# Memory projections: the substitution's last four heads move from GpSimd to VectorE

## What is computed

```
k = k / max(norm(k), 1e-12)
alpha = sigmoid(alpha_raw) * 0.5
def t_step(M, kv):
    Mk = einsum('bhde,bhe->bhd', M, k_t)
    forget = Mk[..., :, None] * k_t[..., None, :]
    write = v_t[..., :, None] * k_t[..., None, :]
    return M - alpha * forget + beta * write
```

## Time and profile before

| | |
|---|---|
| median of three runs | 4661.99 us |
| the profiled execution, its own time | 4658.4 us |
| its span, first to last instruction | 4656.7 us |
| mean granted TensorE clock | 0.885 |
| VectorE busy in the span | 2542.6 us (55%) |
| GpSimd busy in the span | 1687.9 us (36%) |
| the stage, from its first wait to the next stage's first work | about 2541 to 2954 us |

### The profile page before, as it was taken

The page is one execution under the profiler, slowest core; times in us unless marked ns, Lnnn a source line. Parts: engine busy times, 40 slices in busy tenths (PEclk is TensorE's granted clock), DMA queues, the critical chain, the costliest instruction groups (busy, mean ns, idle before and its releaser), DMA issues. The chain is left out here.

```text
span 4656.7 us, 53980 instructions
## 1 busy us (share of the span) xinstructions
PE 3691.3 (79%) x17563; PEld 1661.0 (36%) x17563; DVE 2542.6 (55%) x3976; ACT 1439.1 (31%) x2018; POOL 1687.9 (36%) x1362
## 2 busy tenths in 40 slices
PE   8899999979997899965892330376787966999994
PEld 3322222223333333334551220132445534555553
DVE  5599999935551355534325779655663694111113
ACT  2257777743332233321232210011442210111111
POOL 0132222236663166641560457333441322222221
PEclk9989999989998999987895665687887977999997
DMA  4542232211104411024226111233333103333333
GB/s 172 185 69 68 62 74 63 49 53 37 43 19 134 140 37 37 26 78 133 67 86 214 54 54 36 64 89 95 106 117 110 36 27 101 95 90 104 95 90 81
DMA packets 323882, 382.96 MB, mean 82 GB/s; under 512 B 52016, under 2 KB 252992, under 8 KB 322688
## 3 DMA queue, kind: packets, MB, share of 16 engines
q1 hardware_dynamic: 270912, 285.83, 19.8%
q0 software_dynamic: 35776, 73.97, 6.3%
q10 hardware_dynamic: 17024, 20.97, 1.3%
HBM read 240.69 MB, written 135.76 MB: 81 GB/s over the span
## 5 line engine op out<-in xcount | busy, mean ns | idle before, releaser
L571 DVE TENSOR_REDUCE modulated_mx<-modulated_ring 128x1 f32<-128x512 f32 x1024 | 651.9, 684 | 52.0 <-PE modulated_ring L478 46.4
L555 ACT ACTIVATE modulated_probs<-modulated_scores 128x1024 f32<-128x1024 f32 x512 | 496.1, 1021 | 182.4 <-PE modulated_scores L499 182.3
L2843 DVE TENSOR_TENSOR expert_h<-expert_gelu,expert_bank 128x512 f32<-128x512 f32 x128 | 88.1, 688 | 390.2 <-PE expert_bank L2811 390.2
L2771 POOL DMA_INDIRECT scratch_acc<-expert_y,expert_idx x64 | 101.0, 1579 | 483.7 <-DVE expert_y L2848 441.6
L508 PE MATMUL modulated_acc<-modulated_probs,modulated_v 128*32 128x512 f32 x2048 | 273.6, 606 | 0.6 <-ACT modulated_probs L555 0.6
L499 PE MATMUL modulated_scores<-modulated_q,modulated_k 128*128 128x512 bf16 x1024 | 268.3, 384 | 1.3 <-DMA modulated_q<-modulated_turned 0.7
L478 PE MATMUL modulated_ring<-modulated_k,modulated_q 64*128 64x512 bf16 x1024 | 239.6, 399 | 34.1 <-DMA modulated_v<-scratch_v 22.7
L910 POOL TENSOR_TENSOR causal_total<-causal_total,causal_probs 128x1024 f32<-128x1024 f32 x96 | 225.6, 2350 | 86.5 <-ACT causal_probs L831 85.5
L910 POOL TENSOR_TENSOR meta_total<-meta_total,meta_probs 128x1024 f32<-128x1024 f32 x96 | 225.6, 2350 | 86.6 <-ACT meta_probs L831 85.6
L2811 PE MATMUL expert_bank<-expert_xT,expert_wg 128*128 128x512 f32 x512 | 243.2, 597 | 7.8 <-ACT expert_xT L2823 7.8
L853 DVE TENSOR_REDUCE meta_mx<-meta_maxima 128x2 f32<-128x1024 f32 x120 | 146.0, 1217 | 184.4 <-PE meta_maxima L737 184.4
(11 more groups left out here) (471 smaller groups left out, 7057.2 us busy)
## 6 DMA issues: line engine op xcount, KB each, us to landing
expert_wg<-x_WgT SPq DMA_DIRECT2D x16, 1024.0 KB, 4.8
expert_wu<-x_WuT SPq DMA_DIRECT2D x16, 1024.0 KB, 6.8
expert_wd<-x_WdT SPq DMA_DIRECT2D x16, 1024.0 KB, 5.4
modulated_k<-scratch_k_part SPq DMA_DIRECT2D x192, 64.0 KB, 2.9
modulated_q<-scratch_q_part SPq DMA_DIRECT2D x192, 64.0 KB, 3.0
scratch_v<-proj_v SPq DMA_DIRECT2D x8, 1024.0 KB, 6.6
modulated_v<-scratch_v SPq DMA_DIRECT2D x16, 512.0 KB, 4.4
scratch_M<-steps_snap SPq DMA_DIRECT2D x16, 512.0 KB, 3.2
```

The source lines that it names most:

```text
L555: nc.scalar.activation(probs[u % NPROBS][i][:], sc[i][:], ACT.Exp, scale=SCALE).then_inc(s_exp, 1)
L571: V.tensor_reduce(mx[h % 2][:, x // 2, 1 - j % 2, j // 2, x % 2:x % 2 + 1], ring[bank_of["max", 4 * m + j]][:], AX.X, ALU.max).then_inc(s_ ...
L2771: added[j].done(G.indirect_dma_start(out=scr["acc"], out_offset=bass.IndirectOffsetOnAxis(ap=idx[j][a][:], axis=0), in_=y[j][:, a, :], in_ ...
```

## The change

VectorE's second part becomes all 8 heads of the second half, and GpSimd's third part goes, with its 30 instructions a group, its waits for the copy and for the scaled A, and SP's wait for GpSimd. The number of VectorE's instructions stays; those of the second part have twice the elements.

```
-        pool_s = st.steps("pool", [("far", n) for n in range(len(far))] + [(x, i) for i in range(SUB - 1, 0, -1) for x in ("share", "rows")])
-
-        PARTS = ((0, 0, HP), (1, 0, HP // 2), (1, HP // 2, HP))
+        pool_s = st.steps("pool", [("far", n) for n in range(len(far))])
+
+        PARTS = ((0, 0, HP), (1, 0, HP))
...
                 dve_s.wait(sp, g, ("rows", 1, 1))
-                pool_s.wait(sp, g, ("rows", 1))
                 for half in range(HH):
...
                     pool_s.done(products(nc.gpsimd, other[n % 2], i, hp), ("far", n))
-                act_s.wait(pool, g, "copy")
-                dve_s.wait(pool, g, ("scaled", 1))
-                for i in range(SUB - 1, 0, -1):
-                    pool_s.done(share(nc.gpsimd, other[0], i, PARTS[2]), ("share", i))
-                    pool_s.wait(pool, g, ("share", i))
-                    pool_s.done(add(nc.gpsimd, other[0], i, PARTS[2]), ("rows", i))
-                    pool_s.wait(pool, g, ("rows", i))
```

## The result

The changed kernel took 4641.65 us in the median of five runs (4634.66 to 4644.94), the kernel before, run beside it, 4662.17. The ratio is 0.9941, with a 95% interval of 0.9927 to 0.9956, that is 20 to 34 us less. In a second comparison the medians were 4637.09 and 4668.23 (ratio 0.9941, 0.9927 to 0.9955). Forecast were 32.0 us less, a size inside that interval. The median of 4641.65 itself lies 1.65 us above the high end of the forecast (4640); put as the ratio on the 4661.99 that the forecast started from, it is 4634.5, inside the range.

A forecast was written before the change was run, and what follows sets the result against it. No one engine bounds the program, but VectorE alone bounds the substitution, slowed by GpSimd. 27.0 us from the substitution plus 5.0 from the early load make 32.0, so 4662.0 - 32.0 = 4630.0 us; range 4622 to 4640.

The forecast's parts named there:

- The substitution: VectorE's substitution, all heads on VectorE without GpSimd: 68.2 us a group instead of 81.66, 27.0 us less in both groups.
- The early load: GpSimd's load of the second group's input, issued near 2665 instead of 2738.82, inside the first substitution: worth 5.0 us.
- the landing: Second group's input load, from GpSimd's issue to arrival: 8.6 us as before, so near 2674, inside the substitution.
- ScalarE's wait for the q store: Second group: ScalarE's copy of quad two's q waits some 7 us for the first quad's q store; now comes last.
- the slow restart of TensorE: TensorE idles over 50 us, then starts slowly a second time after the substitution: 1.85 us more on kv matmuls.
- quad three at T + 16.8: TensorE's kv matmuls of the second group's third quad start 16.8 us after the substitution's end (T), instead of 21.8.
- The rival in which the load is starved: GpSimd's early load lands only once VectorE's two-input instructions end: 12.6 us gained in all, 4649; chance 0.02.
- the two terms: VectorE's shorter substitution, 27.0 us in both groups, and the second group's early load, 5.0 us: 32.0 us.
- the 25 to 36 us of the prediction: Sign: wrong if the second substitution's end, counted from the stage's start, comes under 25 or over 36 us earlier.
- Slow long instructions: Substitution rows 15 to 9: long instructions cost 2.01 ns an element by themselves, 47.4 us slower, 4709; chance 0.03.
- A gain given back later in the program: The stage's end waits for something unseen or the next stage starts no earlier: 4662; chance 0.03.

The follow-up runs named there:

- with the order fixed: A wait added so that VectorE's product always goes ahead of GpSimd's next: 4623.92 us on the changed kernel, 4654.26 on the kernel before.
- the second and the third pair of profiles: Both kernels unchanged, each profiled twice more: products of pairs 69.53 to 69.67 us a group in all four executions.
- the first pair: The first profiles of the kernel before and the changed one: memset of A to end of second substitution 397.5 and 379.8 us.
- dve_alone: Changed kernel with VectorE always first, the last four heads' substitution left out, VectorE's old instructions alone: substitution 52.21 us a group, program 4588.60 us.

## Why the prediction was right, and where it was not

**The substitution.** Forecast were 68.2 us, measured 68.20 and 68.21. The price of 1.04 ns an element and 0.07 us an instruction, taken from the short rows that ran alone and from the 1664-element product, holds for the long ones. No row gives the 0.11 us an instruction that the high end of the range allowed for; the long instructions, too, have 0.07. The 29.5 us of waiting that I read out of the trace were 29.45 us when GpSimd's part was simply left out.

**The early load.** Forecast were 5.0 us. By itself it was worth 4.6 us with the order fixed, and 5.7 us between the two traces (5.2 with the order fixed in both). Its steps held: the landing (8.6 us forecast, 8.55 measured), ScalarE's wait for the q store as the new last wait, the slow restart of TensorE (1.85 us forecast, 1.3 measured, and 2.35 with the order fixed: 9.59 us of kv matmuls), quad three at T + 16.8 (16.1 measured). The rival in which the load is starved is gone.

**The rest of the span** is the step that failed. The sum was made against one execution ("The profiled execution took 4658.4 us and would take 4626.4"); everything outside the two terms I took as fixed. It was not: the products of pairs have a short and a long form, 61.8 and 69.6 us a group, and that execution had the short one, which five of six profiled executions did not have. The changed kernel's profile had the long one. That is 15.6 us, and it is why the spans of the two traces differ by only 16.7 us while the substitution alone gave 26.9. This can account for the 11.6 us that 4641.65 lies above 4630. How much of them it does account for is not shown, since the form of an execution without a profile is unknown, and the changed kernel's second five runs, profiled in the same form, gave 4637.09. That the two terms were right and the base was not, the comparisons of like with like show: with VectorE always first in both kernels the change is worth 30.3 us by medians, and 2 x 13.44 + (43.97 - 38.76) = 32.1 us by the traces, where 32.0 were forecast. In the second and the third pair of profiles, both in the long form, the end of the second substitution comes 34.7 and 33.5 us earlier, inside the 25 to 36 us of the prediction; in the first pair it was 17.7. That the ratio of the first comparison still took in the 32.0 us is owed in part to its width, 20 to 34 us. I had a row in hand that points to it, the 128-element product of 2.71 us, though it is the same in both forms. I used it as evidence that GpSimd holds VectorE up, and did not ask whether the next products were let in first by a margin. A rival for it was missing.

**The other rivals.** Slow long instructions: refuted by `dve_alone`. A gain given back later in the program: nothing after the stage did so (from the end of the second substitution to the end of the program 1712.0 us before, 1710.1 after). In the first pair of profiles it was lost inside the stage, ahead of the changed part. The long form occurs without the change; whether the change makes it more frequent, three profiles of each kernel do not tell.

## What to carry to other kernels

Two engines that take turns, instruction by instruction, cost more together than the count of elements tells: here a quarter of the heads on GpSimd cost VectorE 29.5 us a group to save it 16.0. Where such engines still share work, the order of their instructions is better fixed by a wait, which was worth 13 to 14 us here in both kernels: a race of 0.04 us decided some 8 us a group, and no cause for the one or the other outcome stands in either kernel's text. And before a sum is made against one profile, profile the same kernel twice and compare the parts that the change does not touch.

## What was not expected

Two executions of one program differ by 15.7 us in the products of pairs, which wait for no DMA, and no length between the two was seen: 61.8 us or 69.5 to 69.7 us, and the same form in both groups of an execution. A VectorE instruction of 64 elements with a single input, too, was held up by a GpSimd product, for 2.62 us in place of 0.18. The Trainium skill, SBUF — State Buffer, section Who interferes with whom, says that tensor_scalar can take the shared port pair in its two-port mode; this row is in keeping with that, but no trace here shows the mode of an instruction.
